# Small per-head matmuls split into shorter stages, and new instruction orders for all engines

## The reference, cut to what matters

```
h = layernorm(x_tok @ W.T + b) * gamma + beta            # 1024 x 256
h = h + attn0(layernorm(h))    # 16 heads of 64: softcap tanh, causal, gates, w_out 1024 x 256
h = h + tanh(layernorm(h) @ W @ A1 @ A2 + bias)
h = h + attn1(layernorm(h))    # 16 heads of 16: Fenwick mask, proj 256 x 256
h = h + ffn1(layernorm(h))     # w_gate, w_up, w_down with 704 hidden; weights and
                               # activations pass a blockwise FP4 quantise-dequantise
```

## Time and profile before

| what | value |
|---|---|
| time, median of 3 runs | 356.13 us (355.34 to 357.83) |
| the profiled execution's own time | 355.12 us |
| its span, first to last instruction | 353.2 us |
| mean granted TensorE clock | 0.947 of full |
| TensorE matmul busy | 309.1 us (88%), 5122 matmuls and as many weight loads |
| VectorE busy | 242.4 us (69%) |
| ScalarE busy | 115.7 us (33%) |

### The profile page before, as it was taken

How to read it: one execution, slowest core, us unless ns; L and a number is a source line. 1 busy time by engine, 2 the same in 40 slices (tenths; PEclk the granted TensorE clock), 3 DMA queues, 4 the chain that set the end, 5 groups by cost and what they waited for, 6 DMA issues and landing times.

```text
span 353.2 us, 11732 instructions
## 1 busy us (share of the span) xinstructions
PE 309.1 (88%) x5122; PEld 272.3 (77%) x5122; DVE 242.4 (69%) x527; ACT 115.7 (33%) x259; POOL 28.6 (8%) x49
## 2 busy tenths in 40 slices
PE   4589995999996799999998999997889997699585
PEld 3479975999885589998987899886778876578563
DVE  5789975967582454887645887343568888369992
ACT  3743452442432142334241234433213334012121
POOL 1020400000130000100101101000012100110000
PEclk9969996999996889999999999999999999679899
DMA  7992012000100000000000000000000000000001
GB/s 250 369 357 96 0 52 75 2 2 0 61 2 4 5 2 2 2 3 4 17 3 18 4 2 2 0 17 5 5 2 2 15 3 6 2 2 15 0 2 45
DMA packets 8774, 12.80 MB, mean 36 GB/s; under 512 B 779, under 2 KB 5651, under 8 KB 8725
## 3 DMA queue, kind: packets, MB, share of 16 engines
q1 hardware_dynamic: 8724, 12.06, 10.1%
HBM read 11.01 MB, written 1.05 MB: 34 GB/s over the span
## 4 chain that ended last, share of the span: by engine, by line
PE 77%; DVE 11%; issue 8%; DMA 2%; ACT 1%; SPq 0%; ACTq 0%; DVEq 0%
PE psum L1181 69%; PE psum L1359 2%; DMA wqkv_raw<-in_L_attn_w_qkv_dram 2%; PE psum L1381 2%; PE psum L1484 1%; PE psum L1241 1%; DVE qs L802 1%; PE psum L1461 1%; DVE wqkv_lo L820 1%; DVE xT_lo L820 1%; DVE ln_st L869 1%; DVE hhb L805 1%; DVE hhb L812 0%; DVE wq_s L802 0%; DVE hhb L814 0%
## 5 line engine op out<-in xcount | busy, mean ns | idle before, releaser
L538 POOL TENSOR_TENSOR ln_rs<-ln_mv,minus_half 128x1 f32<-128x1 f32 x40 | 27.4, 690 | 287.5 <-DVE ln_mv L872 287.4
L1181 PE MATMUL psum<-aT_hi,wqkv_hi 128*128 128x256 f32 x128 | 37.6, 294 | 0.4 <-DVE aT_lo L820 0.3
L1181 PE MATMUL psum<-aT_lo,wqkv_hi 128*128 128x256 f32 x128 | 36.1, 282 | 0.0
L1181 PE MATMUL psum<-aT_hi,wqkv_lo 128*128 128x256 f32 x128 | 35.9, 280 | 0.0
L553 ACT ACTIVATE qkT<-psum 128x512 f32<-128x512 f32 x32 | 18.9, 598 | 35.0 <-PE psum L1181 35.0
L1181 PE MATMUL psum<-wout_s,oT 128*128 128x256 f32 x128 | 29.3, 382 | 0.0
L1181 PEld LDWEIGHTS psum<-wout_s,oT 128*128 128x128 f32 x128 | 23.8, 190 | 3.3 <-issue 0.2
L1181 PEld LDWEIGHTS psum<-aT_hi,wqkv_hi 128*128 128x128 f32 x128 | 24.1, 188 | 1.7 <-DVE aT_lo L820 0.5
L1181 PE MATMUL psum<-v_aug,probs 32*32 32x65 f32 x1024 | 21.0, 238 | 3.8 <-issue 3.7
L1181 PEld LDWEIGHTS psum<-aT_lo,wqkv_hi 128*128 128x128 f32 x128 | 24.1, 188 | 0.1
L1181 PEld LDWEIGHTS psum<-aT_hi,wqkv_lo 128*128 128x128 f32 x128 | 24.1, 188 | 0.0
(11 more groups left out here) (222 smaller groups left out, 754.2 us busy)
## 6 DMA issues: line engine op xcount, KB each, us to landing
x_in<-in_x_dram SPq DMA_DIRECT2D x4, 512.0 KB, 5.2
wqkv_raw<-in_L_attn_w_qkv_dram SPq DMA_DIRECT2D x4, 512.0 KB, 6.5
wout_s<-in_L_attn_w_out_dram SPq DMA_DIRECT2D x1, 1024.0 KB, 6.9
out_dram<-res SPq DMA_DIRECT2D x8, 128.0 KB, 1.7
wqkv_raw<-in_L_attn_w_qkv_dram SPq DMA_DIRECT2D x1, 768.0 KB, 7.4
w_raw<-in_L_attn_W_qkv_dram SPq DMA_DIRECT2D x1, 768.0 KB, 9.3
wdn_raw<-in_L_ffn_w_down_dram SPq DMA_DIRECT2D x1, 704.0 KB, 8.1
wgu_raw<-in_L_ffn_w_gate_dram SPq DMA_DIRECT2D x1, 640.0 KB, 6.6
```

The lines of the kernel that those rows point to most:

```text
L538: nc.gpsimd.tensor_tensor(ln_rs[:, s, k, j:j + 1], ln_mv[:, s, k, j, 1:2], minus_half[:, :], ALU.pow).then_inc(rstd_ready[f"{k}_{j}"], 1)
L1181: return nc.tensor.matmul(o_, a, b, start=first, stop=last)
```

## The change

`scores` gets a second argument: part 0 makes heads 0 to 7 and waits for four of the `qk` results, part 1 makes heads 8 to 15 and waits for the other four; stage `s{j}` becomes `s{j}0` and `s{j}1`, and only part 0 claims the banks. `mix` becomes three stages of 6, 6 and 4 heads, each of which waits for its own `v{j}{g}`. `mix_done` becomes one semaphore per tile, raised by each part, so that ScalarE's copy of group g waits only for part g of the pass before. `mix1` becomes `mx1a_{j}` and `mx1b_{j}` of 8 heads each. The number of matmuls and weight loads stays as it is; TensorE's list grows from 262 stages to 294. All five orders are replaced.

```diff
 def scores(j, part):
-                    ring1.read_out(pe, i, *[f"qk{m}" for m in range(8)])
-                    banks = [ring1.claim(pe, i, f"s{j}{e}") for e in range(2)]
-                    for hd in range(H0):
+                    ring1.read_out(pe, i, *[f"qk{m}" for m in (2 * part, 2 * part + 1, 2 * part + 4, 2 * part + 5)])
+                    banks = [ring1.claim(pe, i, f"s{j}{e}") if part == 0 else ring1.bank(i, f"s{j}{e}")
+                             for e in range(2)]
+                    for hd in range(part * H0 // 2, (part + 1) * H0 // 2):
...
 def mix(j, part):
-                    ring1.read_out(pe, i, *[f"v{j}{g}" for g in range(3)])
-                    for hd in range(H0):
+                    ring1.read_out(pe, i, f"v{j}{part}")
+                    for hd in range(6 * part, min(6 * part + 6, H0)):
...
-                    last.then_inc(mix_done, 1)
+                    last.then_inc(mix_done[j], 1)
...
 def mix1(j, part):
-                    b = ring2(i).claim(pe, i, f"mx1_{j}")
-                    for hd in range(H1):
+                    b = ring2(i).bank(i, f"mx1_{j}") if part else ring2(i).claim(pe, i, f"mx1_{j}")
+                    for hd in range(part * H1 // 2, (part + 1) * H1 // 2):
...
```

ScalarE and VectorE wait for the parts:

```diff
 def v(j, g):
-                        act.wait_ge(mix_done, 2 * (i - 1) + j + 1)
+                        act.wait_ge(mix_done[j], 3 * (i - 1) + g + 1)
...
 def exp(j):
-                        act.wait_ge(mix_done, 2 * (i - 1) + j + 1)
+                        act.wait_ge(mix_done[j], 3 * i)
...
 def mix_den(j):
-                    dve.wait_ge(mix_done, 2 * i + j + 1)
+                    dve.wait_ge(mix_done[j], 3 * (i + 1))
```

The parts of TensorE's order that matter here, old lines first (each line is cut out of the list, in order; "..." stands for what lies between):

```diff
-  ... qk3.0 aT.1 join_ff2 s0.0
-        turn_gate0 s1.0 mix0.0 qk7.1 qk0.1 qk5.1 v01.1 qk6.1 oT00.0 mix1.0 v11.1 turn_gate1 v10.1 v00.1 oT01.0
...
-        ffn_0.0 out1.0 v12.1 bT_0.0 tok1.2 xT0.3 nT_1.0 qk1_0.0 ffn_1.0 s0.1 val1_0.0 sc1_0.0 s1.1 bT_1.0
-        mix0.1 qk1_1.0 mx1_0.0 val1_1.0 aT.2 sc1_1.0 o1T_0.0 oT01.1 qk0.2 oT00.1 proj_0.0 qk2.2 mx1_1.0 out0.1
...
-        oT11.2 mx1_0.2 out1.2 oT01.3 oT00.3 mix1.3 out0.3 o1T_0.2 oT10.3 oT11.3 proj_0.2 out1.3 nT_0.3 hT0_1.1
-        hT1_1.1 nT_1.2 ffn_0.3 down_1.1 nT_1.3 yT_0.2 ffn_1.2 ffn_1.3 bT_0.3 g0_0.2 u0_0.2 g1_0.2 bT_1.2
-        qk1_0.3 u1_0.2 bT_1.3 qk1_1.2 sc1_0.3 qk1_1.3 sc1_1.2 val1_0.3 sc1_1.3 val1_1.2 mx1_0.3 mx1_1.2
-        o1T_0.3 proj_0.3 val1_1.3 o1T_1.2 mx1_1.3 proj_1.2 o1T_1.3 hT0_0.2 hT1_0.2 proj_1.3 down_0.2 yT_0.3
...
+        v11.0 v01.0 qk3.0 v02.0 v00.0 v10.0 qk0.0 qk6.0 qk7.0 v12.0 qk4.0 qk2.0 xT0.2 aT.1 turn_gate0 s00.0
+        s01.0 join_ff2 turn_gate1 s10.0 s11.0 mix00.0 tok0.2 qk0.1 mix01.0 mix02.0 qk6.1 qk7.1 qk3.1 mix10.0
+        mix11.0 oT01.0 qk1.1 qk2.1 oT00.0 turn_up0 v02.1 out0.0 mix12.0 v01.1 turn_down oT10.0 v12.1 turn_up1
+        oT11.0 xT1.2 nT_0.0 out1.0 ffn_0.0 qk5.1 qk4.1 v11.1 nT_1.0 bT_0.0 s00.1 s01.1 ffn_1.0 qk1_0.0 s10.1
+        val1_0.0 bT_1.0 s11.1 sc1_0.0 qk1_1.0 tok1.2 v00.1 sc1_1.0 mx1a_0.0 mx1b_0.0 v10.1 o1T_0.0 val1_1.0
+        proj_0.0 mx1a_1.0 aT.2 xT0.3 mix00.1 qk1.2 mix01.1 mx1b_1.0 qk6.2 o1T_1.0 qk7.2 yT_0.0 proj_1.0
...
+        v00.2 o1T_0.1 nT_1.1 v10.2 hT1_1.0 proj_0.1 s00.2 down_1.0 s01.2 ffn_1.1 tok1.3 mix00.2 mix01.2 bT_1.1
+        mix02.2 qk1_1.1 s10.2 yT_0.1 s11.2 sc1_1.1 g0_0.1 u0_0.1 aT.3 val1_1.1 mix10.2 mix11.2 qk1.3 g1_0.1
...
+        qk1_0.2 oT00.3 mix10.3 hT0_1.1 oT01.3 mix11.3 hT1_1.1 val1_0.2 out0.3 mix12.3 sc1_0.2 down_1.1 nT_1.2
+        nT_0.3 oT10.3 oT11.3 ffn_1.2 ffn_0.3 out1.3 bT_1.2 mx1a_0.2 mx1b_0.2 qk1_1.2 nT_1.3 bT_0.3 o1T_0.2
+        ffn_1.3 sc1_1.2 proj_0.2 val1_1.2 qk1_0.3 mx1a_1.2 mx1b_1.2 val1_0.3 bT_1.3 o1T_1.2 sc1_0.3 qk1_1.3
+        yT_0.2 proj_1.2 g0_0.2 g1_0.2 mx1a_0.3 mx1b_0.3 sc1_1.3 o1T_0.3 u1_0.2 u0_0.2 proj_0.3 yT_1.2 val1_1.3
+        g0_1.2 g1_1.2 mx1a_1.3 mx1b_1.3 u0_1.2 u1_1.2 o1T_1.3 proj_1.3 yT_0.3 g0_0.3 g1_0.3 hT0_1.2 u1_0.3
+        u0_0.3 yT_1.3 hT0_0.2 hT1_0.2 hT1_1.2 g0_1.3 g1_1.3 u1_1.3 u0_1.3 down_0.2 down_1.2 hT0_0.3 hT1_0.3
+        down_0.3 hT0_1.3 hT1_1.3 down_1.3""",
```

VectorE's order at the start, old and new:

```diff
-        turn_tok split_tokb xT0.0 split_qkv1 split_qkv2 tokA0.0 xT1.0 tokB0.0 split_qkv3 tokC0.0 split_b
-        st1_0.0 tokA1.0 tokB1.0 xT0.1 tokC1.0 ln1_0.0 st1_1.0 split_qkv5 tokA0.1 ln1_1.0 tokB0.1 xT1.1 w0a
-        aT.0 tokA1.1 tokB1.1 split_qkv4 w1a w0b tokC0.1 tokC1.1 split_qkv0 w0c st1_0.1 w0d w0e st1_1.1 w0f
+        turn_tok xT0.0 split_tokb split_qkv0 split_qkv1 split_qkv2 tokA0.0 tokB0.0 xT1.0 tokC0.0 st1_0.0
+        split_qkv4 tokA1.0 ln1_0.0 tokB1.0 tokC1.0 xT0.1 st1_1.0 w0a tokA0.1 ln1_1.0 tokB0.1 xT1.1 split_b
+        aT.0 tokA1.1 tokB1.1 tokC0.1 split_qkv5 w0b st1_0.1 w0c split_qkv3 w0d tokC1.1 ln1_0.1 w0e w1a w0f w0g
```

More of the change, by code:

```diff
@@ new lines @@
+        val1_0.0 bT_1.0 s11.1 sc1_0.0 qk1_1.0 tok1.2 v00.1 sc1_1.0 mx1a_0.0 mx1b_0.0 v10.1 o1T_0.0 val1_1.0
+        proj_0.0 mx1a_1.0 aT.2 xT0.3 mix00.1 qk1.2 mix01.1 mx1b_1.0 qk6.2 o1T_1.0 qk7.2 yT_0.0 proj_1.0
+        mix02.1 g0_0.0 g1_0.0 v01.2 u0_0.0 oT00.1 mix10.1 oT01.1 u1_0.0 mix11.1 v11.2 yT_1.0 out0.1 g0_1.0
+        mix12.1 g1_1.0 u0_1.0 qk4.2 qk3.2 hT0_0.0 u1_1.0 hT1_0.0 oT11.1 oT10.1 nT_0.1 down_0.0 ffn_0.1 tok0.3
+        out1.1 bT_0.1 qk2.2 qk1_0.1 val1_0.1 xT1.3 v02.2 sc1_0.1 v12.2 qk5.2 qk0.2 mx1a_0.1 hT0_1.0 mx1b_0.1
@@ new lines @@
+        v00.2 o1T_0.1 nT_1.1 v10.2 hT1_1.0 proj_0.1 s00.2 down_1.0 s01.2 ffn_1.1 tok1.3 mix00.2 mix01.2 bT_1.1
+        mix02.2 qk1_1.1 s10.2 yT_0.1 s11.2 sc1_1.1 g0_0.1 u0_0.1 aT.3 val1_1.1 mix10.2 mix11.2 qk1.3 g1_0.1
+        oT00.2 qk2.3 oT01.2 mx1a_1.1 v00.3 mx1b_1.1 u1_0.1 o1T_1.1 v11.3 qk0.3 mix12.2 proj_1.1 qk3.3 qk5.3
+        qk7.3 qk6.3 out0.2 yT_1.1 qk4.3 v10.3 v02.3 g0_1.1 s00.3 s01.3 g1_1.1 hT0_0.1 v12.3 oT11.2 u0_1.1
+        oT10.2 u1_1.1 s10.3 hT1_0.1 s11.3 nT_0.2 down_0.1 ffn_0.2 v01.3 mix00.3 mix01.3 mix02.3 bT_0.2 out1.2
@@ L381, in program @@
         second_uses = {f"{u}_{j}": [f"{u}_{j}"] for j in range(2)
-                       for u in ("nT", "ffn", "bT", "qk1", "val1", "sc1", "mx1", "o1T", "proj", "yT",
+                       for u in ("nT", "ffn", "bT", "qk1", "val1", "sc1", "o1T", "proj", "yT",
                                  "g0", "u0", "g1", "u1", "hT0", "hT1", "down")}
+        second_uses.update({f"mx1a_{j}": [f"mx1_{j}"] for j in range(2)})
         prep_uses = {"turn_tok": ["tok_w0", "tok_w1"], "bcast": ["rows"],
@@ L429, in program @@
         exp_done = sem("exp_done")
-        mix_done = sem("mix_done")
+        mix_done = [sem(f"mix_done{j}") for j in range(2)]
         o_ready = sem("o_ready")
@@ L1336, in scores, with mix @@
                 return stage
-            def mix(j):
+            def mix(j, part):
                 def stage(i):
@@ L1439, in scores1, with mix1 @@
                 return stage
-            def mix1(j):
+            def mix1(j, part):
                 def stage(i):
@@ L1452, in stage @@
                                       v1[which(i)][q, j, hd, :], True, True)
-                    last.then_inc(ring2(i).filled(i, f"mx1_{j}"), 1)
+                    if part:
+                        last.then_inc(ring2(i).filled(i, f"mx1_{j}"), 1)
                 return stage
@@ L1502, in _ @@
                 **{f"{s}{j}": f(j) for j in range(2) for s, f in (
-                    ("xT", xT), ("tok", tok), ("s", scores), ("mix", mix), ("out", out_))},
-                **{f"oT{j}{g}": oT_(j, g) for j in range(2) for g in range(2)},
+                    ("xT", xT), ("tok", tok), ("out", out_))},
+                **{f"{s}{j}{h}": f(j, h) for j in range(2) for h in range(2) for s, f in (("s", scores), ("oT", oT_))},
+                **{f"mix{j}{h}": mix(j, h) for j in range(2) for h in range(3)},
                 "aT": aT, **{f"qk{m}": qk(m) for m in range(8)},
```

116 lines of the change are left out of this document (55 added, 61 removed).

## The result

The changed kernel takes 339.91 us (median of 4 runs, 338.14 to 341.33) beside 355.74 us for the kernel before (4 runs on the same chip): ratio 0.955, interval 0.948 to 0.962. The forecast was 342, with a range of 332 to 352. The profiled execution has a span of 337.0 us, 16.2 less than before.

The account below looks back on a forecast made before the run. TensorE was taken as the bound, busy for 309.1 of 353.2 us, its idle time decided by code fetch. 355.1 - 10.1 (up to `out1.3`) - 3.6 (tail) = 341.4 us, stated as 342 (337 to 347), with a range of 332 to 352.

Parts of the forecast that it names:

- Gaps, -14.9: TensorE's "issue" gaps over the whole span: large stages put between small ones save 14.9 us, ends -8 and -20.
- Code fetched in blocks: TensorE's code comes in blocks of 256 instructions; it stands still when through with one before the next has come.
- The walk: Both TensorE lists counted block by block at 3.6 us a block: 21.9 us of gaps in the old, 7.5 in the new.
- The half clock (1.2 instead of 2.4 GHz), -4.1: TensorE's slow clock behind gaps cost 5.1 us up to 272 us; 1 stays, saving 4.1, from 0 to -5.
- Splitting, 0: Stages of half size: matmuls and loads stay at 5122 each, so the split alone saves nothing.
- Waits, +1: Up to 32 more TensorE waits, the nearest releaser at `mix00.0`: +1 us, from 0 to +6.
- The start, +1: VectorE's split_qkv steps ahead of `aT.0` take some 1 us more: +1 us, from -1 to +2.
- Up to `out1.3`, -10.1: Program up to the end of `out1.3`: gaps -11.4, clock -4.1, crossing +3.4, start +1, waits +1, together -10.1 us.
- the crossing: Stages moved across `out1.3` in TensorE's order: 3.4 us more work before it, as much less after.
- The tail, -3.6: Behind `out1.3`, 81.1 us: half of the 5.7 us above its floor given back, 77.5 us, -3.6, from 0 to -6.6.
- the gaps coming back as waits: Rival: with TensorE faster, VectorE's chain comes closer and half of -14 us comes back, 349 us; chance 0.16.
- the slower rival: Rival: sequencer waits hold back the code fetch, so 32 more stages with waits make more blocks slow, 365 us; chance 0.07.

Follow-up runs that it names:

- The split-only kernel: The kernel before with its stages split, the parts back to back at the place of the whole stage, old orders kept: 357.93 us, ratio 1.003.
- the first experiment: The changed kernel with only TensorE's order edited, so that the parts of each scores, mix and mx1 stage run back to back: 350.18 us, ratio 0.984.
- the kernel with four moves: The changed kernel with s11.3, v10.1, tok1.2 and s11.2 moved in TensorE's order, or stages beside them, to fill or empty blocks with gaps: 340.67 us, ratio 0.953.

## Why the prediction was right

*Gaps, -14.9.* Measured 22.4 to 6.7, -15.7. The kernels with the parts back to back confirm that it is the large products between, not the number of stages.

*Code fetched in blocks.* Right, and shown by the shift of 64 instructions. The walk's single block time of 3.6 us was a middle of two things that differ: how soon after a border the packet with the next block starts, and what stands in the DMA queues just then. It predicted the sum and not the places, so the closeness of the sum is in part luck: of the changed kernel's 8 gaps the largest (2.10) is one the prediction did not name, while `s00.0` to `mix00.0`, for which it computed 3.2 us, lost 0.5 (in `mix01.0`, just behind), and `s01.2` to `sc1_1.1` lost 0.5 instead of 1.9. Two readings were slightly off without changing the forecast: the block before 56.92 us took 6.3 us, not 6.1, and one of the 15 gaps (0.36 us at 304 us) stands 16 instructions behind a border.

The 128 KB of the Trainium skill ("Advanced Engine Details and Errata", ISA Cache) fare as they did in the trace of before. The line of 256 instructions holds in every run here. If eight lines were full ahead, doubling `mx1` would hardly have brought 15 us of gaps; the traces look like one block ahead and no more. The prediction left out that the same section of the Trainium skill also says "Only 2 cache lines!". With that reading, the present block and one more, the traces agree; the eight lines were my own division of 128 KB by 16.

*The half clock (1.2 instead of 2.4 GHz), -4.1.* Right in kind; its size in us was not measured by itself. From 60 us to `out1.3` the granted clock was 0.97 before and 0.99 after, in the first 60 us 0.90 and 0.97. Two stretches of the changed kernel, the second behind the gap of 1.25 us in `mx1a_0.0`, the first behind the one of 2.10 us (busy time per engine, then clock):

```profile
230.30:234.00 3.70, 3.70 (x24) 2.78 (x18) 0.41 (x2) 0.94 (x3) 0.00 (x0) 1.00 0.02 4
...
109.00:112.00 3.00, 3.00 (x25) 2.88 (x14) 2.21 (x6) 0.68 (x3) 0.55 (x1) 0.52 0.03 5
```

One fell behind a gap that I had thought short enough, and one did not behind a longer.

*Splitting, 0.* The prediction priced the split itself at nothing ("the split alone saves nothing"). Parts that stand alone don't overlap with each other at their ends, so a price is possible. All of `mix`, in the changed kernel, and in the one with `mix` merged and w_out late (busy, mean ns | idle):

```profile
L1186 PE MATMUL psum<-v_aug,probs 32*32 32x65 f32 x1024 | 19.0, 216 | 0.5 <-issue 0.5
```

```profile
L1190 PE MATMUL psum<-v_aug,probs 32*32 32x65 f32 x1024 | 17.3, 215 | 2.8 <-issue 2.8
```

Same mean, 1.7 us more from the first to the last product of each part. The halves of the scores (0.75 and 0.75 us less 0.07 of overlap, for 1.29) add 0.14 for each of the four stages whose halves stand apart, 0.6 us. But the end of a part overlaps the large stage behind it, which these rows don't count, and TensorE's whole busy time is no longer for it. It is 303.9 us in the changed kernel; the page of the one with `mix` merged and w_out late, at the same mean clock of 0.980, has:

```profile
PE 303.7 (89%) x5122; PEld 265.5 (78%) x5122; DVE 242.8 (71%) x527; ACT 116.0 (34%) x259; POOL 27.9 (8%) x49
```

So 2.3 us is all that these rows allow, and no run shows that the split costs anything. The split-only kernel doesn't decide it either: it has 2.9 us fewer gaps and is no faster, but the clock of its profiled execution was 0.932 where it was 0.947.

*Waits, +1.* `mix00.0`, the stage that the prediction named, waited for nothing. Instead waits for other engines grew by 1.0 us from 28 to 60 us (most of it is the 0.84 us of `s00.0`, waiting for aT_lo) and by 0.8 us in the middle: 1.8 together, inside the 0 to +6. The size was near and the place was wrong.

*The start, +1.* 0: the first product of `qk` began at 28.48 us, before at 28.56.

*Up to `out1.3`, -10.1.* It ended at 262.87, before at 272.13: -9.3. With the measured gaps (17.9 to 5.3, -12.6), waits (+1.8) and start (0), and the clock (-4.1) and the crossing (+3.4) as forecast, the terms give -11.5. The 2.2 us between are not accounted for: the split, or the two terms taken as forecast, may hold them. The forecast was "near 262", so errors in the terms cancelled here.

*The tail, -3.6.* The term that was mis-sized: it lasted 74.1 us, so -7.0. "I give back half" was the step that failed. The floor of 74.5 us, VectorE's list of 67.0 and 7.5 behind it, was the answer. VectorE no longer waits for `proj`, and its wait of 3.0 us for `mx1` (den1b), which ended right behind TensorE's gap of 2.5 us at 308 us, is 0.3 us now. VectorE's waits, before and after:

```profile
DVE den1b L1083 <- PE psum L1181: 3.0, 1, 3.0
```

```profile
DVE den1b L1088 <- PE psum L1186: 0.3, 1, 0.3
```

The stretches of the changed kernel, beside the earlier trace rows:

```profile
262.90:304.00 41.10, 34.20 (x842) 28.07 (x841) 34.83 (x94) 11.36 (x27) 3.80 (x6) 1.00 0.01 3
304.00:330.00 26.00, 22.50 (x110) 18.20 (x111) 25.37 (x50) 5.26 (x15) 0.00 (x0) 0.87 0.00 1
```

VectorE is busy for 34.83 of the first 41.10 us, where it was 29.33 of 42. The tail is 74.0 to 74.4 us in every kernel here that has the new orders, with the parts of `mix` or of all stages back to back too (346.9 - 272.7 in the first experiment), and 80.4 in the old ones with w_out late. The kernel with `mx1` made twice is the exception: 95.7 us, with long gaps in the tail again. So the shorter tail belongs to the order of whole stages, not to the interleaved parts, and it is 7 of the 16 us. Whether it is TensorE's list or VectorE's, which was replaced too, no run separates. The other 9 are mostly the interleaved parts: with them back to back, `out1.3` ended at 272.7 us, near the 272.1 of the kernel before, though with the 3.4 us of work that crossed it.

*The rivals.* Of the gaps coming back as waits, the middle shows 0.8 us and the whole span 4.7, not 7, and those of the tail did not make it longer. That new waits hold back the fetch (the slower rival) has no support: 32 more stages that may wait, and fewer gaps.

## What to carry to other kernels

When an engine stands still in the middle of a stage with nothing to wait for, number its instructions: here gaps at a fixed distance of 256 meant that it was through with its code before the next block was there. What helped was to mix many small instructions with few long ones, and to keep a large load from being asked for just as a burst of small products began; the second is one wait on the queue that issues the load. Price the cure as well: a stage taken early may wait for its operands, as in the kernel with four moves, so the last few gaps may not be worth it.

## What the runs showed of the hardware that I had not expected

- A 1 MB load of 1024 packets held one 16 KB code packet back by 3 us: the border-to-packet time was 4.1 us with it and about 1.0 without (packet at 50.6 us in the run with w_out late), and from the packet to the next matmul it was 2.2 us both times.
- The half clock follows some of the gaps, but not by the gap's length alone: a granted clock of 0.52 behind 1.25 us, 1.00 behind 2.10 us, and behind the same 2.10 us gap of `s11.3` in the kernel with `mix` merged and w_out late 0.59 from 232 to 236 us.
- Sixteen tiny float32 products ahead of the program moved the gap in `s1.0` by 62 instructions: each is four instructions of a block of 256, so 64 such products fill a block.
